# Four-stage gated block: who issues the transfers of the softmax shift rows, ScalarE or SP

## The reference, cut to what matters

```python
x = x + tanh(g_xattn[0]) * xattn0(layernorm(x), ctx, lens)          # stage A
x = x + tanh(g_ffn[0])   * ffn0(layernorm(x))                       # stage B, 3 cycles
x = x + tanh(g_xattn[1]) * xattn1(ctx, layernorm(x), mask, mask)    # stage C
x = x + tanh(g_ffn[1])   * ffn1(layernorm(x))                       # stage D

def xattn1(src, tgt, src_mask, tgt_mask):        # stage C: 8 heads of 32
    key, val = split((src @ W_src.T + b_src) * src_mask[:, :, None])
    q = (tgt @ W_tgt.T + b_tgt) * tgt_mask[:, :, None]
    scores = q @ key.T / sqrt(32)                # per head, 256 x 256
    scores = where(src_mask == 0, -inf, scores)
    update = softmax(scores) @ val
    return concat([tgt, update]) @ W_out.T + b_out
```

## Time and profile before

| | us |
|---|---|
| median of 3 runs | 698.03 (697.13 to 699.14) |
| the profiled execution, its own time | 698.28 |
| its span in the profile | 696.1 |
| PE busy in the span | 657.9 (95%) |
| ACT busy | 452.6 (65%) |
| DVE busy | 428.5 (62%) |
| POOL busy | 202.2 (29%) |
| mean granted PE clock | 0.993 of full speed |

### The profile page before, as it was taken

The page is one execution under the profiler, slowest core; times in us unless marked ns, Lnnn a source line. Parts: engine busy times, 40 slices in busy tenths (PEclk is TensorE's granted clock), DMA queues, the critical chain, the costliest instruction groups (busy, mean ns, idle before and its releaser), DMA issues.

```text
span 696.1 us, 11909 instructions
## 1 busy us (share of the span) xinstructions
PE 657.9 (95%) x3653; PEld 457.6 (66%) x3653; DVE 428.5 (62%) x981; ACT 452.6 (65%) x1204; POOL 202.2 (29%) x299
## 2 busy tenths in 40 slices
PE   5988899999999999699999999999999997799997
PEld 3754555554544447588888888888888875556654
DVE  7973857777765548466767566556665685343522
ACT  7766665535555534667887787788778877646452
POOL 6574424210110012124442342333223230142110
PEclk9999999999999999899999999999999999999999
DMA  8721108501000004433344443433444430001112
GB/s 269 244 96 61 62 31 257 81 1 61 1 0 1 0 1 124 101 87 99 98 113 123 123 116 84 107 93 94 119 122 122 92 80 14 2 1 61 43 49 90
DMA packets 45809, 57.90 MB, mean 83 GB/s; under 512 B 13152, under 2 KB 24258, under 8 KB 45634
## 3 DMA queue, kind: packets, MB, share of 16 engines
q1 hardware_dynamic: 45762, 57.33, 30.4%
HBM read 27.46 MB, written 4.19 MB: 45 GB/s over the span
## 4 chain that ended last, share of the span: by engine, by line
PE 79%; SPq 6%; DVE 3%; ACT 3%; DMA 3%; issue 2%; POOL 2%; DVEq 0%; POOLq 0%; ACTq 0%
PE bank L1197 12%; PE bank L1502 7%; PE bank L1414 6%; PE bank L1432 6%; PE bank L1209 6%; SPq L531 5%; PE bank L1455 5%; PE bank L1645 4%; PE bank L1478 4%; PE bank L1441 4%; PE bank L1495 4%; PE bank L1173 3%; PE bank L1635 3%; PE bank L1177 2%; PE bank L1636 2%
## 5 line engine op out<-in xcount | busy, mean ns | idle before, releaser
L976 ACT ACTIVATE c_junk<-bank,c_nmx 128x256 bf16<-128x256 f32 x256 | 116.6, 470 | 9.3 <-DVE c_nmx L1971 9.2
L1971 DVE TENSOR_REDUCE c_nmx<-bank 128x4 f32<-128x1024 f32 x64 | 75.3, 1219 | 35.7 <-PE bank L1455 35.7
L1197 PE MATMUL bank<-b_o,cw 128*128 128x512 f32 x192 | 90.6, 603 | 1.8 <-ACT b_o L831 1.8
L998 ACT ACTIVATE c_pT<-bank 128x1024 f32<-128x1024 f32 x64 | 62.0, 1017 | 7.0 <-PE bank L1478 5.9
L807 ACT ACTIVATE b_h<-bank,cb 128x512 f32<-128x512 f32 x48 | 32.9, 687 | 51.1 <-PE bank L1197 51.0
L1096 ACT ACTIVATE d_h<-bank,b_col 128x512 f32<-128x512 f32 x64 | 39.6, 686 | 39.3 <-PE bank L1636 39.3
L1197 PEld LDWEIGHTS bank<-b_o,cw 128*128 128x128 f32 x192 | 34.2, 190 | 43.4 <-issue 39.7
L1414 PE MATMUL bank<-c_ctxT,wsrcT 128*128 128x256 f32 x256 | 62.1, 388 | 0.6 <-ACT c_ctxT L957 0.6
L1432 PE MATMUL bank<-wsrcT,c_ctxT 128*128 128x256 f32 x240 | 56.7, 379 | 0.0
L1478 PE MATMUL bank<-c_stack 99*128 99x256 f32 x256 | 47.8, 320 | 7.9 <-DMA c_stack<-c_rows 7.5
L1414 PEld LDWEIGHTS bank<-c_ctxT,wsrcT 128*128 128x128 f32 x256 | 48.6, 194 | 7.2 <-ACT c_ctxT L957 0.9
(11 more groups left out here) (202 smaller groups left out, 1383.0 us busy)
## 6 DMA issues: line engine op xcount, KB each, us to landing
c_stack<-c_parts SPq DMA_DIRECT2D x192, 128.0 KB
a_ctx<-in_ctx SPq DMA_DIRECT2D x16, 512.0 KB, 4.0
c_ctx<-in_ctx SPq DMA_DIRECT2D x16, 512.0 KB, 3.3
out_x<-x_sb SPq DMA_DIRECT2D x7, 512.0 KB, 2.9
x_sb<-in_x SPq DMA_DIRECT2D x3, 1024.0 KB, 11.0
mask_b<-in_mask_BxS_fk SPq DMA_DIRECT2D x1, 2048.0 KB, 12.4
x_sb<-in_x SPq DMA_DIRECT2D x2, 512.0 KB, 5.6
wsrc_raw<-in_L_xattn_W_src SPq DMA_DIRECT2D x1, 1024.0 KB, 7.1
```

The costliest lines, as they stand in the source:

```text
L976: op = nc.scalar.activation(c_junk[:, tc, j, :], scores(tc)[:, j, :], ACT.Exp, bias=c_nmx[hg][:, tc, j:j + 1], accum_out=c_sum[hg][:, tc, ...
L998: nc.scalar.activation(c_pT[hg][:, :, q * S:(q + 1) * S], scores(q), ACT.Exp).then_inc(c_pT_ok, 1)
L1197: op = mm(bank[2 * u + h][:], cw1[:, c, h * P:(h + 1) * P], b_o[n % LANES][:, c, :], start=c == 0, stop=c == DK - 1)
L1971: v.tensor_reduce(c_nmx[hg][:, tc, :], scores(tc), AXIS.X, ALU.max, negate=True)\
```

## The change

SP no longer issues the row transfers, and does not wait for `c_rows_ok`. ACT issues them itself: behind each eviction in `rows_c` it waits until its own eviction is complete and issues the two transfers. `rows_c` on ACT is told the stack's parity for this. On SP the 12 transfers of a stack follow one another without a break. Count, sizes, sources, destinations and semaphores of the transfers stay the same (64 row transfers in all), and PE, DVE and POOL are unchanged.

```diff
@@ SP @@
-            def rows_c(b, s, hg):
-                sp.wait_ge(c_rows_ok, 2 * b + hg + 1)
-                for tc in range(TS):
-                    sp.dma_start(
-                        c_stack[s][MASK_ROW + 1:MASK_ROW + 1 + SHIFTS, 0, :, hg, tc * P:(tc + 1) * P].bitcast(F32),
-                        c_rows[hg][tc * SHIFTS * QH:(tc + 1) * SHIFTS * QH, :].bitcast(F32)).then_inc(c_rows_in, 16)
...
             for b in range(B):
-                if b > 0:
-                    rows_c(b - 1, 1 - b % 2, 1)
                 if b + 1 < B:
-                    stack_c(b + 1, 1 - b % 2, (0, 1))
-                rows_c(b, b % 2, 0)
-                if b + 1 < B:
-                    stack_c(b + 1, 1 - b % 2, (2,))
+                    stack_c(b + 1, 1 - b % 2, range(3))
                     masks_c(b + 1, 1 - b % 2)
                 if b + 3 < B:
                     stream_c(b + 3, 1 - b % 2)
-            rows_c(B - 1, 1, 1)
@@ ACT @@
-            def rows_c(b, hg):
+            def rows_c(b, s, hg):
                 n = 2 * b + hg
                 need(act, c_rows_ps, n + 1)
                 need(act, c_rows_in, 16 * TS * (n - 1))
                 nc.scalar.copy(c_rows[hg][:], bank[6][0:TS * SHIFTS * QH, hg * S:hg * S + P]).then_inc(c_rows_ok, 1)
+                need(act, c_rows_ok, n + 1)
+                for tc in range(TS):
+                    nc.scalar.dma_start(
+                        c_stack[s][MASK_ROW + 1:MASK_ROW + 1 + SHIFTS, 0, :, hg, tc * P:(tc + 1) * P].bitcast(F32),
+                        c_rows[hg][tc * SHIFTS * QH:(tc + 1) * SHIFTS * QH, :].bitcast(F32)).then_inc(c_rows_in, 16)
```

More of the change, by code:

```diff
@@ L1018, in last_c @@
             def last_c(b, s):
-                rows_c(b - 1, 1)
+                rows_c(b - 1, 1 - s, 1)
                 sums_c(b, 0, 0)
@@ L1024, in last_c @@
                 probsT_c(b - 1, 1, 1)
-                rows_c(b, 0)
+                rows_c(b, s, 0)
                 update_c(b - 1, 1 - s, 1)
@@ L1031, in last_c @@
                 probsT_c(b, 0, 1)
-                rows_c(b, 1)
+                rows_c(b, s, 1)
                 update_c(b, s, 0)
```

## The result

The changed kernel takes 732.09 us (median of 4 runs, 731.67 to 732.78) against 697.74 us before (4 runs, 697.13 to 699.14). The ratio is 1.0483, with a 95% interval of 1.0467 to 1.0500: 34 us slower. The profiled execution took 732.12 us, its span is 729.7 us, 33.6 more than before.

A forecast was written before the change was run, and what follows sets the result against it. PE was taken to bound the kernel, busy 239.2 of 240 us in steady stage C. Terms: 12.5 (group 1) + 18.2 + 1.0 (group 0) - 2.5 (first batch) = 29.2 us slower, so 727 us, range 714 to 743.

The forecast's parts named there:

- The price of an issue: On ACT, two row issues were put at 1.33 us with the gap between them, as on SP.
- The hold: ACT is held 1.50 us after each eviction: 0.02 wait, 1.33 for two issues, 0.15 restart.
- The floor of 0.436 for an issue: Quickest issue in the trace, taken as lower bound for ACT's: 0.92 us for two.
- Group 1: Sums start 0.97 us later, 0.83 left after 0.14 slack; 15 times, 12.5 us.
- Group 0: Sums start 1.59 us later, 1.4 left after slack; 18.2 us over batches 1 to 13, 1.0 in batch 14.
- PE does not wait for them in the 240 us: SP's last third and the mask go out about 1.4 us sooner, which gains nothing in steady stage C.
- The first batch: Rows no longer wait behind SP's eight stack transfers; gain of 2.5 us, between 1.7 and 3.1.
- The mask, taken for the limit: Before batch 1's scores, the mask, issued at 292.0, lands 3.71 us later at 295.7 and limits the gain to 3.1.
- a full clock there: Around 292 us in the first batch, PE loses its 4.9 us wait for rows and runs at full clock.
- The end: In batch 15 the last chain runs through group 1's sums, so their 0.83 us delay counts there too.
- Issues that cost nothing: Rival: ACT's issues go out beside its activations, only the first batch and batch 15's mask gain; 694.5 us, 10%.
- Queues that hold each other up: Rival: group 0's ACT issues each wait for an SP stack issue, 0.60 us; 16.8 us more, 745 us, 13%.

The follow-up runs named there:

- The last version: Kernel before, but in batch 0 SP issues group 0's rows behind the first four stack transfers instead of eight; also called the fastest version: 694.46 us.
- the run with group 1 alone: Changed kernel, but ACT issues only the rows of group 1 and SP those of group 0 as before: 712.88 us.
- the run with the issues ahead of the sums: Kernel before plus two unread transfers per batch, issued by ACT directly before group 1's sums; real rows stay with SP: 711.60 us.
- the last rows by SP: Changed kernel, but SP issues the last three pairs of row transfers (group 1 of batch 14, both groups of batch 15): 725.50 us.
- one issue by ACT: Changed kernel, but for each eviction ACT issues one of the two row transfers and SP the other: 707.38 us.
- the wait alone: Kernel before, but ACT also waits for its own eviction of the rows and issues nothing: 699.27 us.
- in the idle slot: Kernel before plus two unread transfers in each of batches 0 to 14, issued by ACT behind update_c; real rows stay with SP: 701.07 us.
- group 0 alone: Changed kernel, but ACT issues only the rows of group 0 and SP those of group 1: 716.35 us.

## Why the prediction was right, and where it was off

The forecast was 727 us in a range of 714 to 743; 732.09 lies in it, on the forecast's side.

- **The price of an issue.** Taken as 1.33 for two from SP's row, 1.27 measured on ACT's own queue. The hold, predicted as 1.50, is 1.50 and 1.49; that it fits so well is partly luck, since the issues took 0.06 less and ACT's restart behind them 0.21 and 0.19 instead of 0.15. The floor of 0.436 for an issue was a misreading: it is the median of its line, whose shortest is 0.382. The forecast does not use it.
- **Group 1.** Its sums start 0.97 later against PE's scores (3.21 us after them instead of 2.24), as predicted. The slack was undersized: 0.83 was to be left, 0.60 to 0.77 was.
- **Group 0.** Predicted 1.4, measured 1.40 to 1.43 over a typical half of 10.15. The period of a typical batch went from 19.85 to between 21.85 and 22.04, not 22.1. Over batches 1 to 13 the sum was 26.2 instead of 29.0 (13 x 0.83 and 18.2); 2.2 of that lies in group 1 (13 x 0.66 measured, by the means) and 0.6 in group 0, where the profiled execution before had two long halves, 10.63 and 10.54. Both end in a wait for the mask, which landed 3.80 and 3.71 us behind its issue:

```profile
418.38 1.21 PE L1455 MATMUL bank<-c_stack 97*128 97x256 f32 x8 [0.41 <-DMA c_stack<-neg_row]
...
438.93 1.21 PE L1455 MATMUL bank<-c_stack 97*128 97x256 f32 x8 [0.33 <-DMA c_stack<-neg_row]
```

  So "PE does not wait for them in the 240 us" was wrong. In the changed kernel PE waits for no mask there, and the sooner transfers give back up to 0.9 us of this execution, a term put at nothing. The last version has no such waits in those batches either, with SP's order of before, so that order alone does not bring them. Batch 14 to 15 was 2.3 where 1.8 was forecast; PE's clock was granted at 0.83 from 600 to 610.
- **The first batch.** Predicted gain 2.5. The scores of batch 1 came 1.56 sooner, of which 0.31 had already been won or lost ahead of the stage (the stack's issues start at 281.56 instead of 281.87): 1.25. I had ACT held for 1.6 and a full clock. ACT was held for 2.0, since its very first issue took 1.26, and PE then waited 2.18 us for the sums and its clock was granted at 0.66, as before. From the last sum (290.55) to the update (296.09) PE needed 5.5 us instead of the 3.1 of the steady stage. The mask, taken for the limit, was not waited for. The step that failed is "a full clock there".
- **The end.** For batch 15 the step was "the chain that ended last runs through these sums themselves, so the delay counts there too", 0.8 us. The delay did count, and brought with it a lower clock for PE: 6.64 us. This is the term that was missing: 5.8 us, and 0.9 more at the first batch (1.56 gained instead of 2.5). The steady stage was put 2.3 too high (2.8 over batches 1 to 13, less 0.5 at batch 14). That these errors cancel in part, so that 732 lies within 5 us of 727, is luck.
- **The rivals.** Issues that cost nothing: excluded, since the sums behind an issue did not start before it had ended; only the eviction ahead of it executed beside it. The rule of the Trainium skill that would have given this rival (Advanced Engine Details and Errata, Sequencer Loop) does not hold for these issues. Queues that hold each other up: excluded in the steady stage, where all of ACT's issues took 0.62 to 0.65; beside SP's own issues of rows the longest took 0.72, far from the added 0.60 of the rival. The other rule of the Trainium skill named in the prediction (Perfetto Trace Analysis, DMA Instruction, HWDGE), that the sequencer is free only at the end of the profiled issue, agrees with the slope of 0.66 to 0.7 for an issue of 0.62.

Left open: why the mask's transfer landed in 2.0 us in the last version and took 3.71 and 3.80 in two steady batches of the kernel before (in the batch of the earlier trace rows it took 3.10), and what exactly brings PE's clock down in one execution and not in the next of the same kernel. The length of the wait alone does not say it: the clock was down after waits of 2.04 us in the changed kernel and 2.08 in the run with group 1 alone, and stayed up after one of 2.00 in the run with the issues ahead of the sums (585.37). Neither was tried.

## What to carry to other kernels

Look for what stands behind an issue on its engine, not at the engine's share of busy time: the same two issues cost 1.4 us ahead of the sums and next to nothing behind an eviction that is followed by a wait. A transfer that already goes out 0.02 us behind its data has nothing to win from another queue; if one pair of transfers in 32 is late, move that one. And where PE already waits now and then at the end of a stage, one more microsecond of waiting can cost several, by the clock (here 0.8 became 6.6, in another run 3.2).

## What the runs showed that I had not expected

- The first issue on ACT's queue takes longer than all others, in each of the seven kernels that have one: 1.26 us against 0.62. In the run with group 1 alone it came at 300.24, with SP idle:

```profile
300.24 1.26 ACTq L994
...
301.54 0.63 ACTq L994
```

- An issue of the same small transfer costs ACT 0.62 us and SP 0.646.
- PE's clock at the end of stage C falls in some executions of kernels that differ by next to nothing there. From the scores of batch 15 to the last output the profiled executions took 24.99 us before, 25.0 with the last rows by SP and with one issue by ACT, 26.5 with the wait alone, 27.3 with the issues ahead of the sums, 27.4 with them in the idle slot, 27.5 with group 0 alone, 27.6 in the fastest version, 28.2 with group 1 alone, 31.6 in the changed kernel. So a fall needs no issue by ACT: the fastest version has none.
